# Adapters per batch fetched by 160 indexed transfers and applied in parts of TensorE's array

## The reference

```python
w = weights[i]; c = einsum('bct,bcd->bdt', x, w) + fside[i][:, :, None]   # 32x32 per batch
x = x + attention(c)            # 16 heads of 16, causal over 32 tokens, W_qkv, W_out

def lora(x, W, A, B):           # A[8, in, 16], B[8, 16, out]
    return x @ W + (x @ A[i]) @ B[i]        # A[i], B[i]: one adapter per batch
h = silu(lora(x, Wg, Ag, Bg)) * lora(x, Wu, Au, Bu)      # 256 -> 1024
y = lora(h, Wd, Ad, Bd)                                   # 1024 -> 256

h2 = fwht(silu(y @ W1.T) * (y @ W3.T))                    # Walsh-Hadamard over 1024
out = x + h2 @ W2.T
```

## Time and profile before

| | us |
|---|---|
| median of 3 runs | 227.52 (227.51 to 227.58) |
| the profiled execution, its own time | 227.53 |
| its span, first to last instruction | 225.7 |
| TensorE busy | 221.0 (98%) |
| GpSimd, ScalarE, VectorE busy | 120.8, 100.2, 85.0 |
| queue q1, SP's: 4,896 packets, 11.72 MB | 16.7% of 16 engines' span |

### The profile page before, as it was taken

One profiled execution on the slowest core, in us unless ns is written; L12 is line 12 of the kernel. 1 busy time (PEld: TensorE's weight loads), 2 busy tenths in 40 slices (PEclk: granted clock), 3 DMA queues, 4 the chain that ended last, 5 costly groups with the idle time before them and its releaser, 6 DMA issues.

```text
span 225.7 us, 3708 instructions
## 1 busy us (share of the span) xinstructions
PE 221.0 (98%) x1485; PEld 178.4 (79%) x1485; DVE 85.0 (38%) x142; ACT 100.2 (44%) x169; POOL 120.8 (53%) x93
## 2 busy tenths in 40 slices
PE   7999998999999999999999999999999999999995
PEld 2577786878788888888888888888888888888894
DVE  4998999898345431210032000203222222220211
ACT  2389799896754325740564000304355555440000
POOL 1029677547786208999999800270266677443000
PEclk9999999999999999999999999999999999999999
DMA  6955500004025001230020000031101100000211
GB/s 180 416 215 180 141 3 4 3 3 139 3 70 159 4 3 15 80 93 26 0 69 24 0 3 0 0 98 42 46 9 47 41 3 0 1 0 0 82 60 46
DMA packets 5345, 13.02 MB, mean 58 GB/s; under 512 B 720, under 2 KB 1360, under 8 KB 5072
## 3 DMA queue, kind: packets, MB, share of 16 engines
q1 hardware_dynamic: 4896, 11.72, 16.7%
q10 hardware_dynamic: 432, 1.07, 1.4%
HBM read 11.73 MB, written 1.05 MB: 57 GB/s over the span
## 4 chain that ended last, share of the span: by engine, by line
PE 86%; ACT 6%; DVE 3%; DMA 1%; issue 1%; POOL 1%; DVEq 0%; ACTq 0%
PE bank L388 27%; PE bank L392 27%; PE bank L390 27%; ACT k_x L682 4%; PE bank L407 2%; PE bank L490 1%; DMA index_i<-index 1%; PE bank L414 1%; ACT k_x L704 1%; DVE k_x L941 1%; ACT prob L698 1%; DVE cond_sel L890 1%; DVE k_x L884 1%; ACT v_tok L692 0%; POOL prob L1170 0%
## 5 line engine op out<-in xcount | busy, mean ns | idle before, releaser
L1183 POOL TENSOR_TENSOR h_lo<-tmp_b,h_hi 128x512 fp32r<-128x512 f32 x32 | 41.1, 1303 | 32.2 <-ACT h_hi L731 32.2
L388 PE MATMUL bank<-act_hi,w_hi 128*128 128x512 f32 x152 | 52.8, 392 | 0.1
L392 PE MATMUL bank<-act_hi,w_lo 128*128 128x512 f32 x152 | 52.4, 389 | 0.0
L390 PE MATMUL bank<-act_lo,w_hi 128*128 128x512 f32 x152 | 52.3, 389 | 0.0
L1029 DVE TENSOR_TENSOR tmp_b<-bank,tmp_a 128x512 f32<-128x512 f32 x32 | 21.1, 688 | 73.6 <-PE bank L392 41.1
L1145 POOL TENSOR_TENSOR w_lo<-raw,w_hi 128x512 fp32r<-128x512 f32 (+3 forms) x22 | 35.9, 1642 | 10.2 <-ACT w_hi L666 10.2
L388 PEld LDWEIGHTS bank<-act_hi,w_hi 128*128 128x128 f32 x152 | 28.5, 188 | 6.9 <-issue 1.1
L392 PEld LDWEIGHTS bank<-act_hi,w_lo 128*128 128x128 f32 x152 | 28.5, 188 | 6.0
L390 PEld LDWEIGHTS bank<-act_lo,w_hi 128*128 128x128 f32 x152 | 28.5, 188 | 5.8
L731 ACT ACTIVATE h_hi<-tmp_b 128x512 fp32r<-128x512 f32 x32 | 19.8, 633 | 27.0 <-DVE tmp_b L1029 27.0
L388 PE MATMUL bank<-h_hi,w_hi 128*128 128x512 f32 (+1 forms) x88 | 27.3, 370 | 0.0
(11 more groups left out here) (88 smaller groups left out, 255.4 us busy)
## 6 DMA issues: line engine op xcount, KB each, us to landing
raw<-w_stream SPq DMA_DIRECT2D x13, 256.0 KB, 2.7
raw<-w_stream SPq DMA_DIRECT2D x8, 384.0 KB, 3.2
raw<-w_stream SPq DMA_DIRECT2D x3, 512.0 KB, 3.7
k_x<-x_slots ACTq DMA_DIRECT2D x2, 512.0 KB, 6.6
tmp_b<-w_t SPq DMA_DIRECT2D x1, 1024.0 KB, 8.9
resid<-x_feat SPq DMA_DIRECT2D x1, 1024.0 KB, 10.6
out_feat<-tmp_b SPq DMA_DIRECT2D x3, 256.0 KB, 2.1
out_feat<-tmp_b SPq DMA_DIRECT2D x2, 128.0 KB, 1.8
```

The lines of the kernel that those rows point to most:

```text
L388: pe.matmul(ps[:, :], w[0], x_hi, start=start, stop=False)
L390: pe.matmul(ps[:, :], w[0], x_lo, start=False, stop=False)
L392: last.append(pe.matmul(ps[:, :], w[1], x_hi, start=False, stop=stop))
L1183: pool.tensor_tensor(lo, tmp_b[:, n % 4, :], f32(hi), ALU.subtract).then_inc(prod_split, 1)
```

## The change

1. **Bias of the conditioning**: the hi and lo parts of fside stand in rows 0 to 7 and 32 to 39 of one array, so one matmul instead of two adds them.
2. **Adapters**: SP reads the indices from SBUF into registers and fetches, batch by batch, that batch's own A and B. a_in: 2 x 16 transfers, each 128 rows x 4 pieces of 64 bytes. b_own (B of gate and up): 64 transfers of 16 rows x 8 pieces of 512 bytes. b_down: 32 of 16 rows x 1 KB. a_down: 32 of 128 rows x 8 pieces of 64 bytes, into memory that b_own0 held, so they wait until up(0, 7) is full. 160 in all, on SP's queue between the weight batches.
3. **Products**: z, zd and the adapter outputs are plain fp32. `adapters_in` multiplies 128 rows x 32 columns (two batches of 16) with 64 tokens in four column parts, 32 products per half; `down_adapters_in` does so for h_hi and h_lo over 8 blocks, 256 products. `adapters_out` multiplies 64 rows x 128 columns with 128 tokens, the upper half of the rows for gate (or d of half 0), the lower for up (or d of half 1): 8 products per pair, 18 pairs. VectorE places z in its slots with two multiplications by 0 and 1 (`own_slots`); ScalarE and GpSimd no longer split z and zd.
4. **Weights**: all batches are 512 columns wide (24 of them), six places in the ring; A and B are no longer among them.
5. **Orders**: all engine lists are rewritten: k and q of the first half run before the second half's conditioning, 7 warm-up matmuls stand between, six blocks run alone for each half and the last two half by half, zd comes between d0 and d1 and its outputs at the middle and the end of d1; GpSimd does one butterfly where it did two.

```diff
         def _(sp):
+            def load_a_in(s, adapter):
+                for b in range(BH):
+                    sp.dma_start(a_in[:, s, :, b, :].unsqueeze(2),
+                                 adapter_cols(P_A, 2 * DC)[:, :, bass.DynSlice(adapter[b], 1), :])\
+                      .then_inc(a_in_loaded[s], 16)
+            def load_b_own(i, g0, adapter, b0, n):
+                for b in range(b0, b0 + n):
+                    rows_ = bass.DynSlice(adapter[b] * R, R)
+                    blocks = w_stream[rows_, PACKED_AT[P_GU]:PACKED_AT[P_D0]].rearrange("r (m a k) -> r m a k", m=HC, a=2)
+                    for a in range(2):
...
+                        sp.dma_start(b_own[i][at:at + R, group], blocks[:, :, a, DC * P:]).then_inc(b_own_loaded[i], 16)
+            def load_a_down():
+                for b in range(B):
+                    if b % 8 == 0:
+                        adapter = adapters(b, 8)
+                    sp.dma_start(a_down[:, :, b, :].unsqueeze(2),
+                                 adapter_cols(P_AD, HC)[:, :, bass.DynSlice(adapter[b % 8], 1), :]).then_inc(a_down_loaded, 16)
...
             sp.dma_start(resid[:, :, :], x_feat).then_inc(resid_loaded, 16)
-            for n in range(STAGES, BATCHES):
-                load_weights(n)
+            sp.wait_ge(index_loaded, 16)
+            first_half, second_half = adapters(0, BH), adapters(BH, BH)
+            load_a_in(0, first_half)
+            load_weights(W_OUT)
+            load_weights(W_GU)
+            load_a_in(1, second_half)
...
+            load_b_own(0, 0, first_half, 0, BH // 2)
+            load_weights(W_GU + 1)
+            load_weights(W_GU + 2)
+            load_b_own(0, BH // 2 // SLOTS, first_half, BH // 2, BH // 2)
+            load_weights(W_GU + 3)
+            load_b_own(1, 0, second_half, 0, BH // 2)
+            for m in range(4, HC):
+                load_weights(W_GU + m)
+            wait_full(sp, "o", 1, 1)
+            load_b_own(2, 0, second_half, BH // 2, BH // 2)
+            load_weights(W_D)
+            load_b_down()
+            for k in range(1, 2 * DC):
+                load_weights(W_D + k)
+            wait_full(sp, "up", 0, HC - 1)
+            load_a_down()
+            for m in range(HC):
+                load_weights(W_F + m)
...
         def _(pe):
-            def adapters_in(s, c, *two):
...
-                    last = both([ps], unit(w, a * DC + c), rows(act_hi, act_lo, c, [s]), c == 0, c == DC - 1)
+            def adapters_in(s):
...
+                for c in range(DC):
+                    for q in range(GROUPS):
+                        for a in range(2):
+                            for e in range(2):
...
+                                last = pe.matmul(ps[64 * a + 32 * e:64 * a + 32 * e + 32, q * 2 * T:(q + 1) * 2 * T],
+                                                 a_in[:, s, a * DC + c, b:b + 2, :].rearrange("p b r -> p (b r)"),
+                                                 resid[:, c, at:at + 2 * T],
...
+            def adapters_out(halves, weight, slots):
+                for q in range(GROUPS):
+                    for h, (name, s, m) in enumerate(halves):
+                        rows_ = slice(64 * h, 64 * h + 64)
+                        ins = pe.matmul(tile(name, s, m)[:, q * P:(q + 1) * P], weight(rows_, q),
+                                        slots[rows_, q].rearrange("p e n -> p (e n)"), start=False,
+                                        stop=True, skip_group_check=True)
...
+            down(0, 0, HC)
+            down_adapters_in()
...
+            down(1, 0, HC // 2)
...
+            down_adapters_out(0)
+            down(1, HC // 2, HC)
+            down_adapters_out(1)
...
         def _(act):
             split_weights(W_K)
             conditioned_hi(0, 0)
-            fold_raw_hi(0, 1, 2)
+            split_weights(W_V)
             conditioned_hi(0, 1)
...
             conditioned_hi(1, 1)
             split_weights(W_OUT)
...
+            split_weights(W_GU)
             queries(0, 1)
...
+            for m in range(0, ALONE, 2):
+                for k in (m, m + 1):
+                    gate(1, k)
+                for k in (m, m + 1):
+                    hidden_hi(1, k)
+                for k in (m, m + 1):
+                    split_weights(W_GU + ALONE + k)
```

More of the change, by code:

```diff
@@ new lines, in adapters @@
+            def adapters(b0, n):
+                _, values = nc.values_load_multi_w_load_instructions(
+                    index_i[0:1, NG + b0:NG + b0 + n], engines=[mybir.EngineType.SP], min_val=0, max_val=N - 1,
+                    skip_runtime_bounds_check_because="an adapter's index lies in 0 to N - 1, as the reference's gather needs")
+                return values
+            def load_a_in(s, adapter):
[3 more added lines that the diff above has]
+                      .then_inc(a_in_loaded[s], 16)
@@ L411, in conditioned_bias @@
                 pe.wait_ge(ones_made, 1)
[L412 to L416, removed]
+                pe.wait_ge(fbias_made, s + 1)
+                full(pe.matmul(tile("xc", s, c)[:, :], ones[:, :], fbias[:, s * BH:(s + 1) * BH, :], start=False,
+                               stop=True, skip_group_check=True), "xc", s, c)
             def projected(name, n, s, m):
@@ L543, in _ @@
             for _ in range(KEEP_WARM):
[L544 removed]
+                pe.matmul(tile("k", 0, 0)[:, :], warm[:, 0:P], warm[:, :], start=True, stop=True)
+            key(0, 0)
+            query(0, 0)
+            key(0, 1)
             conditioned(1, 0)
+            fold(0)
             conditioned(1, 1)
@@ L610, in _ @@
-            for name, n in (("d0", W_D0), ("zd", W_AD), ("d1", W_D1)):
-                w = weights(n)
-                tiles = down[name] = [claim(name, s, 0) for s in range(HALVES)]
-                for k in range(HC):
-                    pe.wait_ge(prod_split, SPLIT_COUNT["up", 1, k])
-                    last = both(tiles, unit(w, k), h_rows(k), k == 0, name == "zd" and k == HC - 1)
-                if name == "zd":
-                    for s in range(HALVES):
-                        full(last[s], name, s, 0)
@@ L619, in _ @@
-            w = weights(W_BD)
-            pe.wait_ge(prod_split, SPLIT_COUNT["zd", 1, 0])
-            for s in range(HALVES):
-                for m, name in enumerate(("d0", "d1")):
-                    last = both([down[name][s]], unit(w, m), rows(aux_hi, aux_lo, 0, [s]), False, True)
-                    full(last[0], name, s, 0)
+                gate_up(m + 1, 1)
+                gate_up_adapters((1, m), (1, m + 1))
+            for s in range(HALVES):
+                for m in range(ALONE, HC):
+                    gate_up(m, s)
+                gate_up_adapters(*[(s, m) for m in range(ALONE, HC)])
@@ new lines, in down, with down_adapters_out @@
+            def down(m, k0, k1):
+                tiles = [tile(f"d{m}", s, 0) for s in range(HALVES)]
+                for k in range(k0, k1):
+                    w = weights(W_D + 2 * m + k // 4)
+                    pe.wait_ge(prod_split, ORDINAL["up", 1, k] + 1)
+                    both(tiles, unit(w, k % 4), h_rows(k), k == 0, k == HC - 1)
+            def down_adapters_out(m):
+                adapters_out([(f"d{m}", 0, 0), (f"d{m}", 1, 0)],
+                             lambda rows_, q: b_down[rows_, q, m * P:(m + 1) * P], zd_slots)
@@ new lines, in down_adapters_in @@
+            def down_adapters_in():
+                ps = claim("zd", 0, 0)
+                pe.wait_ge(a_down_loaded, 16 * B)
+                for k in range(HC):
+                    for part in (h_hi, h_lo):
+                        for q in range(GROUPS):
+                            for s in range(HALVES):
+                                for e in range(2):
+                                    b = q * SLOTS + 2 * e
+                                    last = pe.matmul(ps[64 * s + 32 * e:64 * s + 32 * e + 32, q * 2 * T:(q + 1) * 2 * T],
+                                                     a_down[:, k, s * BH + b:s * BH + b + 2, :].rearrange("p b r -> p (b r)"),
+                                                     f32(part[s][:, k, b * T:(b + 2) * T]),
+                                                     start=(k == 0 and part is h_hi and q == 0),
+                                                     stop=(k == HC - 1 and part is h_lo), skip_group_check=True)
+                full(last, "zd", 0, 0)
@@ L839, in _ @@
+            for m in range(0, ALONE, 2):
[5 more added lines that the diff above has]
+                    split_weights(W_GU + ALONE + k)
+            for s in range(HALVES):
+                for m in range(ALONE, HC):
+                    gate(s, m)
+                for m in range(ALONE, HC):
+                    hidden_hi(s, m)
             act.wait_ge(butterfly, 6)
```

560 lines of the change are left out of this document (285 added, 275 removed), and 25 rows, old and new, of the table EARLY_BANKS.

## The result

The changed kernel takes 245.93 us (median of 4 runs, 243.64 to 247.15) against 227.51: a ratio of 1.0796 (1.0769 to 1.0823). It is slower, where 224.6 was forecast, and 2.9 us above the range. The profiled execution took 247.15 us with a span of 245.0, 19.3 more than before; it is the slowest of the four, 1.2 us above the median. Times in this document are medians of all runs of a kernel, while the ratios and their intervals take only runs within 1.5% of that kernel's fastest.

The account below looks back on a forecast made before the run. TensorE, busy 98% of the span, was taken as the bound. Matmuls -9.4, a_down wait +5.0, clock +1.0, early delay +0.8, earlier products -0.3 made -2.9: 227.5 becomes 224.6 us, range 216 to 243.

Parts of the forecast that it names:

- Matmuls removed and added, -9.4: On TensorE, 180 of 804 matmuls go, saving 40.8 us; the new fp32 adapter products add 31.4 us.
- the case of no concurrency: Rival: row halves or column parts of TensorE's array don't run side by side; 236 to 250 us, chance 0.10.
- zd, 512 passes at 17 ns, 8.9 us: Down adapters' first product on TensorE: 512 passes at 17 ns each plus 0.2 us, 8.9 us added.
- a_down, a wait of 5.0: Before zd, TensorE waits 5.0 us for a_down: 23.5 us of loading against 18.5 us of other work.
- The cover: TensorE's work while a_down loads: two gate_up calls 5.4, an adapter call 2.2, d0 10.9; 18.5 us.
- the middle of SP's queue, nothing: b_own and b_down issues, 53 us of SP over 25 to 105 us, delay nothing, W_D+1 included.
- The early delay, 0.8 with bounds of 0 and 10: a_in(0) behind resid makes W_OUT land about 22 us, delaying ACT's split and the attention chain by 0.8 us.
- The clock after a_down, 1.0: TensorE's clock may fall after idling for a_down: at most 3 us lost, 1.0 taken.
- The rival of SP's pace: Register transfers cost SP 0.8 us each, making a_down and W_D+1 late; 238 us, chance 0.16.
- Small packets at twice the cost: Rival: 64-byte DMA packets take 20 ns each, so a_down's wait is 24.5 us; 249 us, chance 0.16.

Follow-up runs that it names:

- one block: Against the changed kernel, each of the 32 a_down transfers moves only one of its eight k blocks and all zd passes read block 0: 235.07 us.

## Why the prediction was wrong

**Matmuls removed and added, -9.4.** The shapes came out as taken. z takes 1.03 us for 64 passes, 1.2 with the change of shape (forecast 1.3), gate and up 17.4 us busy (17.4), the last output 2.3 (2.5). Column parts on 128 rows and row halves both run side by side; the case of no concurrency, with 0.10, is out. Against the sentence of the Trainium skill on weight loads ("TensorE: Matmul & The Clock Gate", Part 3) stands this trace, for this shape: with all four parts in one row group passes come at 15.5 ns, each with its load.

```profile
L625 PE MATMUL bank<-z_slots,b_own 64*128 64x128 f32 x256 | 17.4, 289 | 0.0
...
L625 PE MATMUL bank<-zd_slots,b_down 64*128 64x128 f32 x32 | 2.3, 285 | 0.0
L604 PE MATMUL bank<-resid,a_in 128*32 128x64 f32 x128 | 2.2, 221 | 0.0
```

**The step that failed first: zd, 512 passes at 17 ns, 8.9 us.** It took 15.6. The rate of 17 ns came from 64 passes in a row, and it is right for 64 and for 128. It was extended to 512 without asking where 1,024 instructions come from; no part of the trace before had so dense a run. The term is 6.7 us short. At full clock throughout zd took 13.4 us (behind d1) and 13.8 (one block), so some 4.7 of the 6.7 stay without the half clock, and these are the gaps. Up to 2 go with the half clock at its start.

**The second: a_down, a wait of 5.0.** It was 10.9. The cover was 17.8 us (118.7 to 136.5), not 18.5. The packets were right, 10.9 ns for 10.5 taken. What was wrong is the sentence that SP's pace "is 21.6 and hides under it". SP's own pace is some 22.0 us by the estimate above, near the 21.6 taken, the packets need 22.2, and together they took 26.1, with the engines 0.85 busy. My reading is that an issue that meets a full engine blocks (up to 1.16 us, against 0.43 free) and SP doesn't catch up on it, so that two limits of nearly one size don't hide under each other. The blocked issues are in the trace; that they are the reason no run has shown by itself.

**The third: the middle of SP's queue, nothing.** "TensorE has about 10 us of banks and weights in hand" looked at W_D+1, where it held. The loss came from W_GU+3 and W_GU+4, each behind sixteen b_own: 1.2 us at 63.9 from the first, 4.0 us at 73 us from the second, and 1.7 us more with the clock at 0.66 from 73 to 78 us. The weights weren't awaited by TensorE but by ScalarE, in front of the attention of half 1. I had listed the issues between o(1,1) and W_D+1 and not those before, though the unbroken run of 48 b_own and 32 a_in lies there.

**The early delay, 0.8 with bounds of 0 and 10.** W_OUT was split at 25.4 us, and not landed near 22. Two a_in issues blocked for 2.4 and 2.8 us behind resid, as named; but from 16 to 22 us, when W_OUT was still behind ten more of them, the DMA engines were 0.57 busy, so it was SP's pace that held it there and not the packets. The wait was 2.9 us from the cadence, and 1.7 more went to the clock (0.76 from 27 to 34 us). The 4.6 lie inside the bounds.

**The clock after a_down, 1.0.** The first 117 passes took 29 ns each at a granted 0.50, 1.6 us more than at 15.5, part of which the supply of instructions would have taken anyway: between 0 and 2 us, as above. The forecast of 1.0 lies within that, which tells no more.

**The sum.** From 225.7: -40.8 for the removed matmuls; +37.4 for those added, zd with its gaps (2.1 + 17.4 + 15.6 + 2.3); +10.9; +4.6 early; +6.9 in the middle: 19.0 of 19.3. That it closes so well is in part luck, since small terms that I left out (0.4 us for z's changes of shape, waits of 1 us and less) don't all cancel for a reason. The rival of SP's pace, 238 us with 0.16, was nearest, and it had the queue right but not the price or the place: free issues cost 0.51 to 0.62 us, not 0.8, and the loss lay ahead of W_GU+3 and W_GU+4, not of W_D+1. Small packets at twice the cost are out: of the read-modify-write below 512 bytes that the Trainium skill states ("DMA: Bandwidth & Descriptors", Specifications) 10.9 ns for 64 bytes shows no cost. The range missed because no case held an instruction limit: without those 6.7 us the time would be some 239.

## What to carry to other kernels

Transfers that replace computation are paid for on the issuing queue: count them, constant or not (0.47 to 0.62 us each here), lay the run of them beside the times at which each engine, not just the critical one, wants what stands behind, and don't count on hiding a run of packets of like size under it (some 22.0 and 22.2 us gave 26.1 here). Spread a dense run of small matmuls between large ones; 64 at a time ran free here, 512 ran at half speed. And where data arrive in order, cut the consumer by arrival along an axis that keeps all parts of the array in use: that turned +8.0% into -0.5% with the same work, and the order of the loads made it -1.0%.

## What the runs showed of the hardware

- A run of small matmuls on TensorE was bounded here at 256 instructions, a 16 KB packet of the instruction queue, in 3.73 us at best (up to 4.6 in the run with zd behind d1): 29 ns for a pass with its weight load. Between 117 and 373 passes went through before the first gap, 373 where more than half of them ran at the half clock. The half clock, 27 to 29 ns a pass, is easily taken for it: the granted clock tells them apart (0.50, and 1.00 in the gaps).
- With a constant address SP's issue is recorded longer (0.51 us for 0.37), and the spacing is nearly that of the register address (0.55 and 0.56, for a_in): the recorded duration alone misleads.
- The spacing of free issues goes with the transfer: 0.53 us for 128 pieces of 64 bytes, 0.62 for 1,024.
- Whether a second queue would issue at the same pace beside SP's wasn't tried.
